# Second attention: products of sums and reciprocals on GpSimd, VectorE's folds behind maxima and low parts

## The reference

```python
x = x + _L0_xattn_ref(_layernorm(x), ctx, mask, ...)   # 16 heads of 16, with biases and mask
x = x + _L0_ffn_ref(_layernorm(x), ...)                # 6 experts, the best 2 of each row
x = x + _L1_xattn_ref(_layernorm(x), ctx, ctx, ...)    # the "second attention"
x = x + _L1_ffn_ref(_layernorm(x), ...)                # piecewise linear GELU, rounded

def _L1_xattn_ref(q, kv, mem, w_q, w_kv, w_concat):    # 16 query heads, one shared key/value head
    c = jnp.concatenate([mem, kv], axis=1)             # here mem and kv are both the context
    qh = (q @ w_q).reshape(B, L, 16, 16).transpose(0, 2, 1, 3)
    k, v = jnp.split(c @ w_kv, 2, axis=-1)
    attn_prob = jax.nn.softmax(jnp.einsum('bhid,bjd->bhij', qh, k) / 4.0, axis=-1)
    out = jnp.einsum('bhij,bjd->bhid', attn_prob, v)
    return out.transpose(0, 2, 1, 3).reshape(B, L, D) @ w_concat
```

## Time and profile before

| | us |
|---|---|
| median of 3 runs (lowest, highest) | 865.36 (864.72, 866.4) |
| the profiled execution, its own time | 866.98 |
| its span | 865.2 |
| busy: PE, DVE, ACT, POOL | 774.8, 659.9, 520.1, 398.4 |
| second attention, first score to first score of block 15 | 445.2 to 611.3 |

### The profile page before, as it was taken

How to read it: one execution, slowest core, us unless ns; L and a number is a source line. 1 busy time by engine, 2 the same in 40 slices (tenths; PEclk the granted TensorE clock), 3 DMA queues, 4 the chain that set the end, 5 groups by cost and what they waited for, 6 DMA issues and landing times.

```text
span 865.2 us, 13721 instructions
## 1 busy us (share of the span) xinstructions
PE 774.8 (90%) x4452; PEld 568.9 (66%) x4452; DVE 659.9 (76%) x1576; ACT 520.1 (60%) x942; POOL 398.4 (46%) x323
## 2 busy tenths in 40 slices
PE   4799999999899999999988988988879999899996
PEld 3456556666467787777754544554458888788885
DVE  7657877777768777877777888888777778787784
ACT  3455565555554455544446675666668787788774
POOL 5523322223233433443311221222159998988995
PEclk9999999999999999999988999999999999999999
DMA  6965643355200000001075446555000000000001
GB/s 216 159 164 109 146 78 72 74 107 102 70 0 1 2 3 5 2 1 50 15 97 70 59 60 110 88 75 75 3 1 1 25 1 26 25 25 2 25 25 50
DMA packets 24817, 48.01 MB, mean 55 GB/s; under 512 B 3655, under 2 KB 6856, under 8 KB 24234
## 3 DMA queue, kind: packets, MB, share of 16 engines
q1 hardware_dynamic: 23224, 46.02, 27.8%
q10 hardware_dynamic: 1522, 1.11, 0.4%
HBM read 11.47 MB, written 4.19 MB: 18 GB/s over the span
## 4 chain that ended last, share of the span: by engine, by line
PE 52%; DVE 18%; POOL 11%; issue 7%; ACT 5%; DMA 5%; POOLq 0%; ACTq 0%; DVEq 0%
PE bank L135 15%; PE bank L396 5%; PE bank L371 5%; PE bank L629 5%; PE bank L421 5%; DMA qst<-mt 4%; PE bank L407 4%; DVE mx L327 4%; POOL eex L508 4%; PE bank L777 4%; POOL fy L696 3%; POOL frise L689 3%; PE bank L399 2%; PE bank L121 2%; DVE x L597 2%
## 5 line engine op out<-in xcount | busy, mean ns | idle before, releaser
L301 ACT ACTIVATE pt<-bank 77x512 f32<-77x512 f32 x256 | 146.4, 589 | 123.5 <-PE bank L399 76.4
L327 DVE TENSOR_REDUCE mx<-bank 128x4 f32<-128x308 f32 x256 | 108.9, 471 | 30.3 <-PE bank L374 17.8
L396 PE MATMUL bank<-qst,l_kst 128*77 128x512 f32 (+1 forms) x256 | 106.7, 431 | 19.3 <-DMA qst<-mt 13.3
L696 POOL TENSOR_TENSOR fy<-fpart,fg 128x512 f32<-128x512 f32 x64 | 103.9, 1624 | 9.4 <-DVE fpart L737 4.8
L371 PE MATMUL bank<-l_kblk,qh 128*128 128x308 f32 x256 | 89.7, 366 | 12.0 <-DVE mx L327 9.8
L689 POOL TENSOR_TENSOR frise<-fg,fg 128x512 f32<-128x512 f32 x64 | 90.1, 1408 | 9.0 <-POOL fy L696 4.7
L103 POOL TENSOR_TENSOR rstd<-var,minus_half 128x4 f32<-128x4 f32 x32 | 33.2, 1039 | 127.6 <-DVE var L98 74.9
L396 PEld LDWEIGHTS bank<-qst,l_kst 128*77 128x77 f32 (+1 forms) x256 | 36.8, 148 | 83.2 <-issue 48.8
L277 POOL TENSOR_TENSOR ol<-ot,oh 128x512 fp32r<-128x512 f32 x32 | 43.0, 1345 | 94.2 <-ACT oh L306 62.1
L371 PEld LDWEIGHTS bank<-l_kblk,qh 128*128 128x128 f32 x256 | 49.3, 193 | 55.9 <-issue 46.8
L737 DVE SCALAR_TENSOR_TENSOR fpart<-ffixed,frise 128x512 f32<-128x512 uint16 x64 | 58.6, 915 | 33.0 <-POOL frise L689 32.8
(11 more groups left out here) (179 smaller groups left out, 2144.2 us busy)
## 6 DMA issues: line engine op xcount, KB each, us to landing
qst<-qh SPq DMA_DIRECT2D x64, 256.0 KB, 6.7
qst<-ql SPq DMA_DIRECT2D x32, 256.0 KB, 9.0
out<-x SPq DMA_DIRECT2D x8, 512.0 KB, 2.6
qst<-ml SPq DMA_DIRECT2D x8, 480.0 KB
x<-in_x SPq DMA_DIRECT2D x3, 1024.0 KB, 12.7
weights<-in_mlp_w SPq DMA_DIRECT2D x2, 1024.0 KB, 5.1
mraw<-in_mask SPq DMA_DIRECT2D x8, 154.0 KB
x<-in_x SPq DMA_DIRECT2D x2, 512.0 KB, 5.5
```

The lines of the kernel that those rows point to most:

```text
L301: self.nc.scalar.activation(self.pt[0:T, i // 4 % 2, i % 4, :], self.bank_of(G, i)[0:T, :], ACT.Exp).then_inc(self.probs, 1)
L327: self.nc.vector.reduce_max(out, banks[u % len(banks)][:, 0:4 * T].rearrange("q (p par t) -> q p par t", p=2, par=2), AX.X).then_inc(self. ...
L396: last = self.nc.tensor.matmul(out, layer.kst[rows, layer.stack(c * HC + 2 * k + par), b * T:(b + 1) * T], self.qst[rows, self.slot(G), c ...
L696: self.nc.gpsimd.tensor_tensor(self.y[:, k % 2, :], self.part[:, k % 2, :], self.g0[:, k % self.R, :], ALU.add).then_inc(self.y_ready, 1)
```

## The change

`divide` is split in two: `invert` (transposition of U and reciprocals, on VectorE) and `multiply` (the product, on the engine that is named). In the second attention GpSimd does the product (`quotient`), followed by a wait for itself; the first attention still uses `divide`. GpSimd's order in a block becomes: product of quarter 3 of p, `norm.invert`, the two `ol` of p, products of quarters 0, 1 and 2 of G, then the weight splits. `invert` waits, before it writes half q % 2 of `ut`, for the product of two quarters earlier. VectorE's `fold(p, 1)` moves behind maximum 6, and `fold(G, 0)` behind the norm's two low parts.

```diff
+    def quotient(self, pool, G, q):
+        self.multiply(pool, self.nc.gpsimd, G, q)
+        pool.wait_ge(self.divided, 4 * G + q + 1)
...
-    def divide(self, dve, G, q):
-        nc = self.nc
-        c, par = divmod(q, 2)
+    def invert(self, dve, G, q):
         k = 4 * G + q
         dve.wait_ge(self.weighed, k + 1)
-        nc.vector.transpose(self.ut[:, q % 2, :], self.U[:, :]).then_inc(self.unfolded, 1)
+        need(dve, self.divided, k - 1)
+        self.nc.vector.transpose(self.ut[:, q % 2, :], self.U[:, :]).then_inc(self.unfolded, 1)
...
+    def multiply(self, who, engine, G, q):
+        c, par = divmod(q, 2)
+        who.wait_ge(self.inverse_ready, 4 * G + q + 1)
+        need(who, self.folded, C * (G - 1) + c + 1)
+        group = self.ut[:, q % 2, :].rearrange("p (j d) -> p j d", d=32)
+        engine.tensor_tensor(self.o32[:, c, :, par, :], group[:, :, 0:DH],
+                             self.rden[:, q % 2, :, :].to_broadcast([P, N // 32, DH]), ALU.mult).then_inc(self.divided, 1)
...
                 for G in range(BLOCKS, 2 * BLOCKS):
+                    if G > BLOCKS:
+                        att.quotient(pool, G - 1, 3)
                     norm.invert(pool, LN_ATT1 + G - BLOCKS + 2)
                     if G > BLOCKS:
                         for c in range(C):
                             att.rest_quotient(pool, G - 1, c)
+                    for q in range(3):
+                        att.quotient(pool, G, q)
...
+                att.quotient(pool, 2 * BLOCKS - 1, 3)
                 for c in range(C):
                     att.rest_quotient(pool, 2 * BLOCKS - 1, c)
...
                     if p >= BLOCKS:
-                        att.divide(dve, p, 3)
+                        att.invert(dve, p, 3)
+                    if n < 2 * BLOCKS:
+                        att.take_maxima(dve, n, range(4, 7), att.X)
+                    if p >= BLOCKS:
                         att.fold(dve, p, 1)
                     if n < 2 * BLOCKS:
-                        att.take_maxima(dve, n, range(4, 10), att.X)
-                    att.divide(dve, G, 0)
+                        att.take_maxima(dve, n, range(7, 10), att.X)
+                    att.invert(dve, G, 0)
...
-                    att.divide(dve, G, 1)
-                    att.fold(dve, G, 0)
+                    att.invert(dve, G, 1)
                     if nm <= LN_FFN:
                         for c in range(C):
                             norm.rest(dve, nm, c, att.W[c], att.xh if nm < LN_FFN else ff.xh[0], att.xl if nm < LN_FFN else ff.xl[0])
+                    att.fold(dve, G, 0)
```

More of the change, by code:

```diff
@@ L328, in take_maxima, with divide @@
                                       AX.X).then_inc(self.max_taken, 1)
-    def divide(self, dve, G, q):
-        nc = self.nc
-        c, par = divmod(q, 2)
+    def invert(self, dve, G, q):
         k = 4 * G + q
         dve.wait_ge(self.weighed, k + 1)
-        nc.vector.transpose(self.ut[:, q % 2, :], self.U[:, :]).then_inc(self.unfolded, 1)
+        need(dve, self.divided, k - 1)
+        self.nc.vector.transpose(self.ut[:, q % 2, :], self.U[:, :]).then_inc(self.unfolded, 1)
         dve.wait_ge(self.unfolded, k + 1)
         group = self.ut[:, q % 2, :].rearrange("p (j d) -> p j d", d=32)
[L338 to L341, removed]
+        self.nc.vector.reciprocal(self.rden[:, q % 2, :, :], group[:, :, DH:DH + 1]).then_inc(self.inverse_ready, 1)
+    def multiply(self, who, engine, G, q):
[5 more added lines that the diff above has]
+                             self.rden[:, q % 2, :, :].to_broadcast([P, N // 32, DH]), ALU.mult).then_inc(self.divided, 1)
+    def divide(self, dve, G, q):
+        self.invert(dve, G, q)
+        self.multiply(dve, self.nc.vector, G, q)
     def fold(self, dve, G, c):
@@ L1385, in _ @@
                             norm.rest(dve, nm, c, att.W[c], att.xh if nm < LN_FFN else ff.xh[0], att.xl if nm < LN_FFN else ff.xl[0])
+                    att.fold(dve, G, 0)
                     if n == 2 * BLOCKS:
                         ff.early(dve, 0)
-                    att.divide(dve, G, 2)
+                    att.invert(dve, G, 2)
                     if n == 2 * BLOCKS:
                         ff.early(dve, 1)
-                att.divide(dve, 2 * BLOCKS - 1, 3)
+                att.invert(dve, 2 * BLOCKS - 1, 3)
                 att.fold(dve, 2 * BLOCKS - 1, 1)
```

## The result

| | before | after |
|---|---|---|
| median (lowest to highest), runs | 865.19 us (864.41 to 866.99), 9 | 869.15 us (867.26 to 872.82), 9 |
| the profiled execution: own time, span | 866.98, 865.2 | 867.47, 865.7 |
| second attention, first score to GpSimd's first difference behind it | 445.20 to 634.87: 189.67 | 442.80 to 636.03: 193.23 |

The ratio is 1.0047, 95% interval 1.0028 to 1.0066: slower by about 4 us. The forecast was 869.1. The profiled pair of executions differs by only 0.5 us. In it the second attention takes 3.56 us more; the part ahead of it is 2.40 shorter and the feed-forward 0.66, where the two kernels do the same work. Ahead of the stage TensorE's granted clock was 0.99 in the changed kernel's execution and 0.98 in the other, and TensorE was busy 398.2 us in place of 402.5 with as many matmuls, so the 2.40 lies in the pair of executions and not in the change.

What follows compares the result with a forecast made beforehand. TensorE and VectorE were taken as interlocked, with the distance from reciprocal to output deciding. Costs of 3.8, 1.85 and 0.4 less gains of 0.4, 0.8, 0.3 and 0.8 gave +3.75 on 865.36: 869.1 us, range 866.6 to 872.0.

Steps and rivals of the forecast that it cites:

- The product's price: One product of 256 elements on GpSimd: 0.65 us, scaled from a 231-element row, bounds 0.59 and 1.28.
- Rival (2): Products on GpSimd in groups of 16 out of 32 run at half speed, 1.28 us each: 874.1 us, chance 0.13.
- The chain: Blocks 9 to 14, quarter 3's reciprocal to the output through GpSimd's new order: 5.04 us against 4.41, +0.63 a block.
- The second path: `fold(p, 1)` behind maximum 6 starts 1.6 us later, delaying `oh` and second `ol`: +0.6 even with a free product.
- The delay goes on whole: Everything behind the output hangs on TensorE's order, so blocks 9 to 14 each lose the full 0.63: +3.8 us.
- rival (3): No change to be told: output's delay partly made up, as maxima 10 and 11 are ready; 866.4 us, chance 0.14.
- (b): Products no longer caught in GpSimd's weight splits: -0.8 us in block 10, -0.3 in blocks 12 and 13 together.
- (c): Block 11's low parts lose a product and a fold ahead of them, so block 12's queries start earlier: -0.8 us.
- (a): Block 8, without p or output: TensorE's wait for maximum 10 loses the product of 0.42 ahead of it, -0.4 us.
- The signs of being wrong: Waits at `output` absent, or ScalarE, doing `oh` later and ahead of exponential 6, making scores 9 or 10 wait.
- Block 15: No maxima there; reciprocal 0.2 us later, then GpSimd's 5.04 us to the output: +1.85; the stretch behind it +0.4.
- Rival (1): Faster: VectorE's relief counts and the chain on GpSimd doesn't; 862.9 us, chance 0.08.

Runs made afterwards that it cites:

- filler15: The changed kernel plus twelve matmuls of 128 x 512, results unread, in TensorE's wait for `ol` in block 15: 867.89 us, 1.0032 of before.
- root_first: The changed kernel with the norm's root and shift ahead of the product of quarter 3 on GpSimd: 867.02 us, 1.0016 of before.
- ol_first: The changed kernel with root, shift and first `ol` ahead of the product of quarter 3 on GpSimd, also in block 15 and behind it: 869.77 us, 1.0048.
- fold_after5: The changed kernel with only `fold(p, 1)` moved, behind maximum 5 instead of 6: 871.18 us, 1.0059 of before.
- folds_only: The kernel before with only the two folds in their new places, all products on VectorE: 870.22 us, 1.0061 of before.
- products_only: The changed kernel with both folds back in their old places, products on GpSimd: 871.45 us, 1.0076 of before.
- block15_vector: The changed kernel with block 14's product of quarter 3, done in block 15, back on VectorE: 865.99 us, 1.0013 of before, one run left out.
- best: The changed kernel, fold behind maximum 5, GpSimd's first `ol` ahead of quarter 3's product, that product on VectorE for the last two blocks: 859.04 us, 0.9926 of before.
- ol_first_fold5_again: Second timing of the changed kernel with fold behind maximum 5 and GpSimd order root, first `ol`, product of quarter 3, second `ol`: 863.65 us, 0.9984 of before.
- the version with both edits: The changed kernel with fold behind maximum 5, and root and first `ol` ahead of quarter 3's product on GpSimd: 861.90 us, 0.9957 of before.

## Why the prediction was right, and where not

Right were the sign and the mechanism that the forecast named. The size is right too, but by errors that cancel. The forecast's terms, beside the same stretches of the two profiled executions (us, after minus before):

| stretch | predicted | measured |
|---|---|---|
| block 8 | -0.4 | -0.03 |
| blocks 9 and 10 | +1.26 - 0.8 = +0.46 | -0.15 |
| blocks 11 and 12 | +1.26 - 0.8 - 0.15 = +0.31 | -0.20 |
| block 13 | +0.63 - 0.15 = +0.48 | +0.35 |
| block 14 | +0.63 | +0.40 |
| block 15, to the first difference behind it | +1.85 + 0.4 = +2.25 | +3.19 |
| sum | +3.73 | +3.56 |

The sum was right partly by luck: blocks 8 to 14 cost 0.37 where 1.48 were predicted, and block 15 cost 0.94 more.

How much luck, filler15 shows. In its profiled execution TensorE's low clock falls in the same blocks as in the kernel before, 8 and 9, with the same mean in block 8 (0.85). Its stage takes 191.83 us, 2.16 more than before. That is what the terms of the forecast, which had no low clock in them, come to with the clock alike, where 3.73 was predicted. The low clock in block 15 adds 1.27, and that was in no term.

**The product's price**: 0.622 on the mean of 32, predicted 0.65. Rival (2), half speed, is out.

**The chain**: 4.98, predicted 5.04; the wait for `ol` 0.43 to 0.54 (0.21 in block 10), a little under the 0.6 to 0.8 that I named. From block's start to first output blocks 10, 11 and 14 take 0.55 longer, predicted 0.63. Shown by the runs: root_first and ol_first take GpSimd's part of it away, fold_after5 the other.

**The second path**: predicted at +0.6 with a free product, it is +0.4 (4.81 in folds_only against 4.41). The fold starts 1.88 behind the reciprocal's end (571.84 against 569.96) where it started 0.50 behind, so 1.38 later, not 1.6.

**"The delay goes on whole"** is the step that failed in part. With maxima 10 and 11 ready, no output has to wait for a max unit between the two: they stand 2.01 to 2.03 apart in every block without a low clock, where before it was 2.14 in the best case. In block 14 the two max units ahead of the second output take 0.63 us in the trace before (from 602.21) and 0.45 in the changed kernel's (from 600.37). So block 14, without a split, gives back 0.13 of the 0.55, and costs 0.40. That was the argument of rival (3), which I had put at 0.14; it is true, but for a quarter of the delay, not for most of it.

**The gains.** (b) Product and split no longer meet: in filler15, block 10's outputs stand 2.03 apart, 0.95 less than before, predicted 0.8; blocks 12 and 13 gain 0.30 each, where I had 0.3 for both. (c) Block 12's queries no longer wait for low parts. Blocks 11 and 12 lose 1.1 by the chain and gain 0.13 + 0.30 by the outputs; with -0.20 measured, 0.87 is left for (c), predicted 0.8. The trace before agrees: from the block's start to the first output block 12 takes 13.35 us where blocks 10, 11 and 14 take 12.49 to 12.50; in the changed kernel it takes 13.00 where they take 13.04 to 13.05. No run isolates (c), but products_only, with the fold back ahead of the low parts, has the wait again. (a) Block 8's 0.4 doesn't show in the pair: TensorE waits 0.63 for a maximum in place of 1.15, and the block takes 22.50 against 22.53. Both have a mean clock of 0.85 there, and where in the block it is low differs. In filler15, block15_vector and best, which do the same in block 8 and have the mean of 0.85 too, it takes 22.21 to 22.23: 0.3 less than before, so (a) is worth about 0.3. In root_first, ol_first_fold5_again and products_only, where the mean is 0.92, it takes 21.4.

**The signs of being wrong** didn't show: the waits at `output` are there, and TensorE's scores waited for ScalarE once, for 0.2 us, in both kernels.

**Block 15** is the term that was mis-sized. The chain's part is +1.64 (predicted 1.85) and the tail's +0.28 (0.4). Missing was +1.27 between the outputs: a wait of 3.18 us is not only its own length. The clock fell to its lower level, and the twelve matmuls behind it ran at it. filler15's trace shows it: the same chain, no low clock, 1.25 us less between the outputs. By the Trainium skill, "TensorE: Matmul & The Clock Gate", Part 1, the array falls to 1.2 GHz when it has been idle and gets 2.4 GHz back only after it has been kept busy; the trace agrees, 0.50 behind the wait and 0.85 over 620 to 622. I had this wait in the prediction, as "3.5 us in block 15", and had not asked what came behind it.

**The clock elsewhere.** TensorE has stretches at the lower level in blocks 8 to 14 too, in the kernel before as well (0.76 over 478 to 482). In which block they fall differs between kernels that do the same there: filler15 has its outputs 3.27 apart in block 9, the changed kernel 3.16 apart in block 10. That hides, in the table above, what blocks 9 and 10 each cost. The nine runs of the changed kernel nearly order themselves by it, from 867.26 us at a mean granted clock of 0.981 to 872.82 at 0.969. The medians of the clock were 0.975 for the changed kernel, for fold_after5, folds_only and products_only, 0.981 or 0.982 for the kernel before, 0.979 for best. So a part of the 4 us is probably this clock in the repeated runs. That part isn't shown: how large it is, and why the waits of 0.2 to 0.5 us a block that the change brings should bring such stretches, was not isolated. filler15 shows it for block 15 alone.

Rival (1), that VectorE's relief counts, was wrong for this change and right for the version with both edits. The relief is real, but comes only where the output doesn't wait for the moved work: blocks 13 and 14 take 22.74 and 22.51 us in best, against 23.38 and 23.24 before, all at a clock of 1.00. Blocks 9 and 10 take 22.41 each against 24.53 and 24.02, but there a low clock (block 9) and a split (block 10) are gone as well.

## What to carry to other kernels

When work moves to an engine with room, what counts is not its price there but what stands between it and the one who needs it: write down the new order on both engines, and follow every path to the consumer, since two paths of nearly equal length hide each other and each edit alone seems useless or harmful. Blocks at the edge of a pipeline, where nothing covers a wait, want their own placement: here the product of quarter 3 belonged on GpSimd in six blocks and on VectorE in the last two. A wait of some microseconds on TensorE is to be priced with the low clock that may follow it. And where stretches at the low clock fall in other places from run to run, compare stages in which they fall alike, or say that they don't.

## What the runs showed of the hardware

- A product of 128 x 256 elements in groups of 16 out of 32, with a spread second operand, takes 0.62 to 0.63 us on GpSimd (32 of them, mean 0.622) and 0.42 to 0.43 on VectorE when GpSimd does nothing large beside it.
- VectorE's product has two operands in SBUF. Where it starts while GpSimd is in an `ol` or a weight split (two inputs, 512 elements), its record lasts until 0.28 to 0.29 behind the end of GpSimd's: 14 of 14 cases in the second attention of before and folds_only (1.51 us in folds_only, 1.27 in before). Where the product starts first, it takes its 0.42 (before, 492.39, with a split from 492.63 on), and GpSimd's root over 4 elements didn't hold it either (before, 614.76). The Trainium skill, "GPSIMD Engine Reference", section 1, has the two engines share their SBUF interfaces, with contention for VectorE's instructions with two SBUF inputs; the trace agrees. VectorE's maxima, which read PSUM, are not held: two take 0.83 us beside an `ol` (572.47 in the changed kernel).
- The clock behind a wait of TensorE isn't told by the wait's length alone: behind 1.6 to 1.7 us it stayed at 1.00 in before, folds_only's outputs (1.73 apart) and best, and fell to 0.50 in the profiled execution of block15_vector; behind the waits of 2.38 (root_first) to 3.75 us (ol_first) it fell in each profiled execution. With the filler in the wait it did not.
- After 3.73 us of wait (ol_first_fold5_again) the low clock lasted over both outputs, 0.50, 0.50 and 0.75 in three windows of 2 us; after 3.18 us (the changed kernel) over the first only.
